# A decoder layer in fp32: the first normalisation's transposes move from TensorE to VectorE, a tile ahead

## The reference, cut to what matters

```
x = x + attn(layernorm(x))            # blocks of 128 rows, one head of 512, causal, softmax
x = x + xattn(layernorm(x), ctx)      # 16 heads of 32, silu(scores * mask) in place of a softmax
x = x + ffn(layernorm(x))             # gelu(z @ w1 + b1) @ w2 + b2, 512 -> 2048 -> 512
```

## Time and profile before

| | |
|---|---|
| median of 3 runs | 1269.65 us (1269.42 to 1270.09) |
| the profiled execution | 1269.33 us, span 1266.9 us |
| TensorE busy | 1250.7 us (99%), granted clock 1.0 |
| VectorE, ScalarE, GpSimd busy | 665.5, 487.4, 244.3 us |
| DMA | 60.04 MB, mean 47 GB/s |

### The profile page before, as it was taken

One profiled execution on the slowest core, in us unless ns is written; L12 is line 12 of the kernel. 1 busy time (PEld: TensorE's weight loads), 2 busy tenths in 40 slices (PEclk: granted clock), 3 DMA queues, 4 the chain that ended last, 5 costly groups with the idle time before them and its releaser, 6 DMA issues.

```text
span 1266.9 us, 15607 instructions
## 1 busy us (share of the span) xinstructions
PE 1250.7 (99%) x5785; PEld 1039.4 (82%) x5785; DVE 665.5 (53%) x1210; ACT 487.4 (38%) x887; POOL 244.3 (19%) x225
## 2 busy tenths in 40 slices
PE   9989999999999999999999999999999999999998
PEld 7878888888888888867888888888888888888887
DVE  7476858585858585856733443333424334433211
ACT  7246555545454545444332222322222322223221
POOL 2303232323232313138601002001001010020000
PEclk9999999999999999999999999999999999999999
DMA  8210202020202020316210010010100100100000
GB/s 294 81 63 13 76 14 75 13 75 12 75 12 75 12 75 12 125 40 210 75 67 1 1 67 1 1 66 0 36 30 0 66 0 0 66 0 0 34 1 34
DMA packets 40486, 60.04 MB, mean 47 GB/s; under 512 B 4224, under 2 KB 14464, under 8 KB 40448
## 3 DMA queue, kind: packets, MB, share of 16 engines
q1 hardware_dynamic: 40448, 59.53, 14.1%
HBM read 41.17 MB, written 18.35 MB: 47 GB/s over the span
## 4 chain that ended last, share of the span: by engine, by line
PE 54%; DMA 1%; SPq 0%; DVE 0%; ACT 0%; issue 0%; DVEq 0%
PE bank L50 18%; PE bank L52 18%; PE bank L51 18%; DMA w_raw<-in_w 0%; DMA x_dram<-resid 0%; DVE resid L1166 0%; SPq L1049 0%; DVE w_parts L185 0%; ACT w_parts L181 0%; SPq L1047 0%; SPq L189 0%; SPq L1046 0%; DVEq L1165 0%; SPq L1056 0%
## 5 line engine op out<-in xcount | busy, mean ns | idle before, releaser
L1156 DVE TENSOR_TENSOR hid_lo<-gelu_out,hid_hi 128x512 fp32r<-128x512 f32 x128 | 98.2, 767 | 399.1 <-ACT gelu_out L1123 399.0
L50 PE MATMUL bank<-zT,w_parts 128*128 128x512 f32 x768 | 299.3, 390 | 4.9 <-DVE zT L150 1.8
L52 PE MATMUL bank<-zT,w_parts 128*128 128x512 f32 x768 | 298.8, 389 | 0.0
L51 PE MATMUL bank<-zT,w_parts 128*128 128x512 f32 x768 | 298.8, 389 | 0.0
L1119 ACT ACTIVATE hid_hi<-bank,b_col 128x512 fp32r<-128x512 f32 x128 | 88.3, 690 | 491.0 <-PE bank L52 491.0
L50 PE MATMUL bank<-w2p_hi,hid_lo 128*128 128x512 f32 x512 | 199.3, 389 | 0.7 <-DVE hid_lo L1156 0.7
L52 PE MATMUL bank<-w2p_hi,hid_hi 128*128 128x512 f32 x512 | 199.2, 389 | 0.0
L51 PE MATMUL bank<-w2p_lo,hid_hi 128*128 128x512 f32 x512 | 199.2, 389 | 0.0
L50 PEld LDWEIGHTS bank<-zT,w_parts 128*128 128x128 f32 x768 | 144.2, 188 | 36.7 <-issue 3.0
L51 PEld LDWEIGHTS bank<-zT,w_parts 128*128 128x128 f32 x768 | 144.2, 188 | 29.8
L52 PEld LDWEIGHTS bank<-zT,w_parts 128*128 128x128 f32 x768 | 144.0, 188 | 29.9
(11 more groups left out here) (141 smaller groups left out, 1811.0 us busy)
## 6 DMA issues: line engine op xcount, KB each, us to landing
x_in<-in_x SPq DMA_DIRECT2D x32, 256.0 KB, 3.7
x_dram<-resid SPq DMA_DIRECT2D x32, 256.0 KB, 2.1
w_raw<-in_w SPq DMA_DIRECT2D x32, 256.0 KB, 3.4
resid<-x_dram SPq DMA_DIRECT2D x32, 256.0 KB, 3.1
out_dram<-resid SPq DMA_DIRECT2D x32, 256.0 KB, 2.1
resid<-in_wqkvT SPq DMA_DIRECT2D x12, 256.0 KB, 4.8
mask_i<-in_mask SPq DMA_DIRECT2D x16, 128.0 KB, 2.6
values_now<-values_dram SPq DMA_DIRECT2D x8, 256.0 KB, 2.8
```

The source lines that it names most:

```text
L50: pe.matmul(out_ap, lhs[1], rhs[0], start=start, stop=False)
L51: pe.matmul(out_ap, lhs[0], rhs[1], start=False, stop=False)
L52: return pe.matmul(out_ap, lhs[0], rhs[0], start=False, stop=stop)
L1156: dve.tensor_tensor(hid[1][:, c % 4, :], gelu_out[:, c % 2, :], f(hid[0][:, c % 4, :]), ALU.subtract).then_inc(hid_lo, 1)
```

## The change

Tile a + 1's first normalisation is made in step (a, b) instead of tile a's: its input comes by four more DMAs a step (`load_ahead`) into buffers that stand empty until the feed-forward part; its statistics are taken one step earlier still; VectorE writes its rows (`rows_ahead`) behind the low parts of the cross keys, turns them with 16 transposes of 32 rows that are spread over the step (`turn`), and at the start of the next step ScalarE and VectorE split the turned rows, from SBUF and no longer from PSUM. `transposed_chunks` stays for tile 0 alone. GpSimd adds the output bias after the rows ahead are written, and has the 8 `silu_low` behind it in a row. The banks are dealt out anew.

The last step has another order on all engines; its four residual additions are moved into the feed-forward block; b1 and b2 are loaded at the start of the attention block; one gelu on one column is put ahead, in the last step. `small` and `bias_cols` are made 512 bytes wide (before, `bias_cols` had 128), so that all large buffers start at 128 modulo 512 bytes; the buffers allocated behind it (`yv`, `act_in`, `part`, `prob`, `probT`) started at 256 modulo 512.

```diff
 # setup, sync engine, behind the 12th weight chunk
                                 for i in range(NB):
                                     load_x(sp, 0, i)
+                                load_ahead(sp, 1)
 # setup, vector engine
                         for n in range(20, WO_CHUNK):
                             split_low(n)
+                        stats_ahead(dve, 1, range(NB))
+                        aggregate(dve, 1, mv1, ln1)
                         dve.wait_ge(bias_loaded, 64)
 # attention, sync engine
+                            if twice_more(a):
+                                sp.wait_ge(z1_ready, NB * (a + 2))
+                                load_ahead(sp, a + 2)
 # attention, gpsimd
-                            if b is not None:
-                                norm_rstd(pool, mv1, ve1, rstd1, ln1, a)
-                                for j in range(4):
-                                    silu_low(b, j)
-                            pool.wait_ge(z1_ready, NB * (a + 1))
-                            for i in range(NB):
+                            if more(a):
+                                pool.wait_ge(z1_ready, NB * (a + 2))
+                            for i in range(NB):
+                                pool.wait_ge(x_loaded[i], 16 * (a + 1))
                                 pool.tensor_tensor(x_in[:, i, :], x_in[:, i, :], bout_row[:, :], ALU.add
                                                    ).then_inc(x_biased, 1)
...
+                            if twice_more(a):
+                                norm_rstd(pool, mv1, ve1, rstd1, ln1, a + 2)
 # attention, vector engine
+                        def turn(a, first_turn, count):
+                            if more(a):
+                                for n in range(first_turn, first_turn + count):
+                                    dve.transpose(*squares(n, z1_cols)).then_inc(z1_turned, 1)
...
                                 for m in range(EC):
-                                    q_low(b, m)
-                                for c in range(EC):
-                                    chunk_low(dve, a, c, 4)
-                                mask_and_values(b)
+                                z1_low(a, 0)
+                                q_low(b, EC - 1)
+                                for c in range(1, EC):
+                                    z1_low(a, c)
...
+                            else:
+                                rows_ahead(1, None)
+                                dve.wait_ge(values_stored, 16 * BATCH)
+                                dve.nop(nofuse=True)
+                                turn(a, 0, 2)
+                            turn(a, 2, 2)
                             for m in range(EC):
-                                low(yv, m, 4 + m, y_hi, y_lo, EC * a + m + 1)
-                            for i in range(NB):
+                                low(yv, m, m, y_hi, y_lo, EC * a + m + 1)
+                                if m == 2:
+                                    turn(a, 4, 2)
+                            turn(a, 6, 4)
+                            for i in range(NB):
+                                if i == 2:
+                                    turn(a, 10, 2)
...
+                            turn(a, 12, 2)
...
+                            turn(a, 14, 2)
                             dve.wait_ge(pT_hi, a + 1)
 # attention, tensor engine
                                 queries(b, range(EC))
-                                transposed_chunks(pe, a, 4)
...
 # feed-forward, vector engine, tile 0
+                            if splits_weights(t) and c == 0:
+                                for i in range(NB):
+                                    second_residual(dve, TILES - 1, i, (TILES - 1) % 2, LAST_PROJ_BANK)
```

More of the change, by code:

```diff
@@ L25 @@
 SQUARE = 32
[L26 to L39, removed]
+LINE = 128
+VALUE_BANK = (5, 6, 7, 0)
+SELF_BANK = (4, 3)
+PROB_BANK = 5
+KEY_BANK = (7, 0)
+SCORE_BANK = (4, 5, 6, 7, 1, 2, 3, 4)
+OUT_BANK = (7, 0, 1, 5)
+BLOCK_BANK = (2, 3, 4, 6)
+PROJ_BANK = (7, 0, 1, 5)
+LAST_SCORE_BANK = (6, 7, 4, 5, 2, 6, 3, 4)
+LAST_OUT_BANK = (7, 6, 4, 6)
+LAST_PROJ_BANK = (0, 1, 2, 7)
+FIRST_BANK = (0, 1, 5, 3)
 def decoder_layer_program(nc, x, ctxT, mask, wqkvT, woutT, b_out, xwqT, bq, xwkT, bk, xwvT, bv, xwoT,
@@ L96, in decoder_layer_program @@
         minus_half = sb("minus_half", [P, NB])
+        small = sb("small", [P, LINE])
+        b1_col, gelu_table = small[:, 0:FC], small[:, FC:FC + 1]
+        b2_row = sb("b2_row", [P, E])
         x_loaded = [sem(f"x_loaded{i}") for i in range(NB)]
@@ L219, in decoder_layer_program @@
             values_stored, wo_lo = sem("values_stored"), sem("wo_lo")
-            values = [w2_raw[:, b, :] for b in range(STAGES)]
-            values.append(w1_raw[:, 0, :, :].rearrange("p c n -> p (c n)"))
+            z1_cols = sb("z1_cols", [P, EC, TILE])
+            values = [z1_cols[:, b, :] for b in range(BATCH)]
+            ahead = [w1_raw[:, i, :, :].rearrange("p c n -> p (c n)") for i in range(STAGES)]
+            ahead.append(w2_raw[:, 0, :])
+            ahead_loaded, z1_turned = [sem(f"ahead_loaded{i}") for i in range(NB)], sem("z1_turned")
             RAWS = 2 * NB
@@ L482, in first, with more, twice_more @@
                     return isinstance(t, int) and t == 0
+                def more(a):
+                    return not (isinstance(a, int) and a == TILES - 1)
+                def twice_more(a):
+                    return not (isinstance(a, int) and a >= TILES - 2)
                 with nc.Block() as block:
@@ L554, in step @@
                             if b is not None:
-                                for j in range(4, 8):
+                                for j in range(8):
                                     silu_low(b, j)
@@ L722, in mask_and_values, with mask_now @@
+                        def mask_now(b):
                             dve.wait_ge(mask_loaded, 32 * (b + 1))
@@ L876, in queries @@
                             for m in chunks_:
-                                if m == 1 and not first(b):
-                                    pe.wait_ge(x2_ready, NB * b)
+                                if m < 2 and not first(b):
+                                    pe.wait_ge(x2_ready, NB * b - 2 + m)
                                 project(m, lambda c: at(wq, c, cols(m)), lambda c: at(zT, c), q_done)
@@ L925, in step @@
                             for i in range(NB):
-                                last = pe.transpose(bank[1][:, cols(i)], prob[:, i, :], ident[:, :])
+                                last = pe.transpose(bank[PROB_BANK][:, cols(i)], prob[:, i, :], ident[:, :])
                             last.then_inc(pT_done, 1)
@@ L1186, in down @@
                         pe.wait_ge(hid_lo, FC * t + c + 1)
-                        if c == 0 and not splits_weights(t):
+                        if c == 0 and splits_weights(t):
+                            pe.wait_ge(x2_ready, NB * TILES)
+                        elif c == 0:
                             pe.wait_ge(out_ready, NB * t)
```

239 lines of the change are left out of this document (146 added, 93 removed).

## The result

| | before | changed |
|---|---|---|
| median of 6 runs | 1269.87 us (1269.42 to 1270.62) | 1274.76 us (1273.53 to 1275.39) |
| ratio | | 1.0039, 95% interval 1.0029 to 1.0049 |
| profiled execution, span | 1269.33, 1266.9 | 1274.43, 1272.6 |

The account below looks back on a forecast made before the run. TensorE, busy in 99% of the span, was taken as the bound, with VectorE's chain deciding the loop tile. Terms summed to +0.25 us, giving 1269.9 us, no change the runs could tell from zero; range 1261 to 1275.5, the forecast's own 1267.4 to 1272.4.

Parts of the forecast that it names:

- Setup (+4.1): Before tile 0: added loads and VectorE's 2.9 us of statistics start tile 0 4.1 us late; bounds 2.0 and 5.5.
- step 6 (+2.0): Step 6: VectorE's four rows take 5.9 us beside GpSimd's additions, z2 2.4 us late; with the tile's gain, +2.0.
- step 7 (-1.8): Step 7: no transposes of either kind, so VectorE's chain follows TensorE; 1.8 us gained.
- last step (-3.3): Last step and block end: new order gains 2.5 us, TensorE not leaving behind VectorE's four additions 0.8 us.
- feed-forward start (-2.2): Feed-forward start: TensorE's waits go, as b1, b2 are there and chunk 3's loads not behind stores; 2.2 us gained.
- The loop tile: Steps 2 to 6: TensorE 1.78 us earlier at y, but VectorE's chain leaves a tile gain of 0.42 us.
- Tile 0 (+3.15): Tile 0: a pair of transposes ahead of probT, 1.45 us, and statistics ahead of z2's low parts, 1.7 us, add 3.15.
- Step 1 (0): Step 1: gains 1.8 us up to y as its own waits go, pays 1.5 and 0.3 later: nothing.
- The first (a period of 61.4): Loop tiles: transposes are hidden, steps 1 to 6 each gain 1.78 us: 1261.7, or 1265.8 with half; chance 0.34.
- the third (over 63.2, by longer transposes): Loop tiles: VectorE becomes the bound; at 0.08 us more per transpose 1275.7, at 0.05 1273.5; chance 0.20.
- The second: Last step: its gain doesn't come, GpSimd's low parts stay at 1.3 us each; 3.3 us more, 1273.2; chance 0.09.
- the sum of +0.25: Whole kernel: all terms against the profiled execution add up to +0.25 us, span from 1266.9 to 1267.15.

Follow-up runs that it names:

- e4: Changed kernel with GpSimd's four bias additions of tile 7 put behind the first low part of its step's queries: 1272.04 us.
- e5: Changed kernel with tile 1's four loads behind setup's last weight chunk, its statistics and aggregation at tile 0's start: 1269.59 us.
- e12: Changed kernel with tile 7's residual additions back in the last step, b1 and b2 loaded in the feed-forward block, no gelu ahead: 1277.04 us.
- e3: Changed kernel with turns 4 and 5 behind the last low part of y and not ahead of it: 1273.38 us.
- e1: Changed kernel with 14 matmuls into an unused bank in each of three TensorE waits (setup's end, tile 0, ahead of step 1): 1271.32 us.
- e11: Changed kernel with e3's, e4's and e5's edits, the mask made at a step's start, tile 0's turns and statistics moved: 1263.06 us, ratio to before 0.9947.
- e9: Changed kernel with three of z1's four low parts on GpSimd, later bias additions, y's products reordered, setup and tile 0 work moved: 1283.26 us.
- e8: Changed kernel with e3's and e4's edits, e5's loads, all statistics ahead at a step's start, turns 14 and 15 moved: 1268.30 us, ratio to before 0.9989.
- e7: Changed kernel with bias_cols 128 bytes wide again, so five buffers start at 256 modulo 512 bytes as before: 1273.63 us.

## Why the prediction came out as it did

- **Setup (+4.1), step 6 (+2.0), step 7 (-1.8), last step (-3.3), feed-forward start (-2.2)** are right within 0.3 us. The cause is shown for step 6 (e4), for setup as a whole (e5), for 0.7 us of the block's end and for most of the feed-forward start (e12); step 7 and the new order of the last step rest on the walk through the order alone. The rows of step 6 took 5.78 us where 5.9 were taken, and not 7.4, as if each row had waited for a whole addition. Setup's terms as they are written (1.0 + 1.1, then 2.9 - 1.27) add up to 3.7 and not to 4.1: TensorE's last matmul of setup came 1.7 us later and its wait behind that grew by 2.3.
- **The loop tile.** The mechanism is right: a wait of 1.1 us ahead of the self scores (0.95 to 1.05 in steps 2 to 5), a transposed pair ahead of the last low part of y, and e3 moves the wait along the chain. Its size is off: 0.07 us a tile (steps 2 to 5), not 0.42. In step 2 TensorE comes 1.69 us earlier to y, counted from the step's first matmul (1.78 in the prediction), 0.55 earlier to the self scores (0.73), 0.20 earlier to prob @ v (0.42) and 0.16 earlier to the next step. What is lost on the way are restarts: a matmul behind even a short wait is issued 0.1 us late, and from issue to issue the changed step has 0.1 more at the queries' start and at y's, 0.21 ahead of prob @ v and 0.08 behind its first matmul. I had counted such a restart at the one large wait alone. Step 4 then takes 0.12 more than before, at the loop's turn.
- **Tile 0 (+3.15).** Here a term was missing. Waits alone are +3.2 (e1: 43.77 against 40.60); the other 3.2 us are two stretches at half clock. In the earlier trace rows the clock stood at 1.0 behind waits of 1.6 and 1.8 us, and I let three waits grow to over 3 us without asking what the clock does behind a longer one. The kernel before waits no longer than 1.84 us once tile 0 has begun, so its trace could not have told the price. But that the clock falls was there to be seen: behind its last matmul, at 1263.16, TensorE has no work left, and from 1266.14 to the end the clock stands at half.

```profile
1266.20:1266.80 0.60, 0.00 (x0) 0.00 (x0) 0.00 (x0) 0.00 (x0) 0.00 (x0) 0.50 0.00 0
```

So it should have stood in the range as an unknown. The two waits of tile 0 themselves grew by 1.60 and 1.55 us from issue to issue, 3.15 in sum, as forecast.
- **Step 1 (0)** came out at +0.67, with the third low stretch absorbed. That its own waits go was wrong: with the clock at 1.0 TensorE waits 1.26 us at y (e1). Its wait at the self scores is 1.48 us, 0.5 more than in steps 2 to 5. What the 0.67 is made of was not tested.
- **Rivals.** The first (a period of 61.4) and the third (over 63.2, by longer transposes) are both wrong: the period is 63.0 and a pair of transposes takes 1.44 us. The second did not come. Why the change came out slower and not equal: the sum of +0.25 lacked 3.2 of clock, 1.4 in the loop and 0.7 in step 1, together 5.3 of the 5.5 by which the span missed.

The sum of stages is +5.7 and the medians differ by 4.9. Most of that is the time around the span, which the prediction took as unchanged: 2.43 us in the kernel before, 1.8 in every run of the changed one. Why it is shorter was not asked.

That the measured time lies in the stated range is luck in part. The range reached up to 1275.5 for transposes that take longer (the third rival), and they didn't; the clock, which filled that room, was no term of it.

## What to carry to other kernels

When work moves to a less busy engine, its busy share says whether it fits; the stretch in which that engine has no wait says what it costs. Here 0.42 us taken out of that stretch gave the critical engine 0.3 to 0.4 (e11). A wait of the critical engine is not priced by its length alone: ask whether the clock falls behind it, and whether another wait stands ready to absorb that. Place VectorE's subtractions, conversions and scalings from SBUF to SBUF where GpSimd is idle, and check this for each new neighbour, also of work that was not moved; its transposes and statistics could stand beside GpSimd here.

## What the runs showed of the hardware

- TensorE's granted clock fell to 0.5 for 3.4 us (in places 6.8) around or behind 24 of the 26 waits of 3.05 us and more that the traces hold behind setup's last matmul. Length alone doesn't decide: e3 and e5 kept 1.0 at waits of 3.29 and 3.17 us at which the changed kernel lost it, and e11 at one of 2.84; in e9 it fell at two of five waits of 2.24 to 2.29, and in e11 behind one of 1.25 with two of 0.53 and 0.30 ahead of it. What decides was left open.
- VectorE beside GpSimd, both on SBUF: four low parts of the cross values went from 1.23 us to 3.31 and 4.21, the mask from 0.42 to 1.42, four normalised rows from 1.92 to 5.78. Not all work on SBUF suffers: in the changed kernel 61 transposes beside GpSimd took 0.70 us each, as the others did, and in e9 four statistics beside its additions and low parts took 0.68, as alone. Operations that read PSUM took 0.69 either way.
- At the turn of a hardware loop VectorE stood for 2.62 us (e8) and 2.51 us (e11) with nothing to wait for. Step 4 took 2.8 us more than its neighbours in e8, 0.7 in e11, and 0.2 to 0.3 in the changed kernel, e1, e3 to e7 and e12. In the changed kernel VectorE stood for 2.40 us there, 0.9 of which it waits in the other steps too.
